# Graph-network kernel, edge-maximum passes: three TensorE signals a step and nine one-hot buffers

## The reference, cut to what matters

```
x = x + attention(relu(layernorm(x)), src, dst)      # stage 1
x = x + pooled_sage(relu(layernorm(x)), src, dst)    # stage 2: two layers
x = x + weighted_sum(relu(layernorm(x)), src, dst)   # stage 3
x = x + propagate(relu(layernorm(x)), src, dst)      # stage 4: 16 steps

# one layer of stage 2 (3125 nodes, 50000 edges sorted by dst, 96 features)
m = relu(x @ Wp + bp)
agg = segment_max(m[src], dst)                       # the edge maximum
return x @ Ws + agg @ Wn + b
```

## Time and profile before

| what | value |
|---|---|
| median of 3 timed runs | 2830.38 us (2829.44 to 2841.82) |
| the profiled execution, its own time | 2817.04 us |
| its span, first to last instruction | 2815.3 us |
| TensorE busy, share of the span | 2462.9 us, 87% |
| VectorE busy | 1766.1 us, 63% |
| ScalarE busy | 1151.0 us, 41% |
| GpSimd busy | 1130.3 us, 40% |
| granted TensorE clock, mean | 0.903 of 2.4 GHz |

### The profile page before, as it was taken

The page is one execution under the profiler, slowest core; times in us unless marked ns, Lnnn a source line. Parts: engine busy times, 40 slices in busy tenths (PEclk is TensorE's granted clock), DMA queues, the critical chain, the costliest instruction groups (busy, mean ns, idle before and its releaser), DMA issues. The chain is left out here.

```text
span 2815.3 us, 72099 instructions
## 1 busy us (share of the span) xinstructions
PE 2462.9 (87%) x29232; PEld 1986.4 (71%) x29232; DVE 1766.1 (63%) x5033; ACT 1151.0 (41%) x2585; POOL 1130.3 (40%) x1407
## 2 busy tenths in 40 slices
PE   6998999986888888677887888469899999999999
PEld 4666777754555555445555565359899999999999
DVE  6997999986777777545776777320444444444444
ACT  5997888864444444423444444310311111111110
POOL 4007999974666666446666666320000000000000
PEclk7558999997999999888998999569999999999999
DMA  5103000013545555533554555549200000000000
GB/s 164 41 2 102 13 12 12 13 61 86 140 127 132 132 131 139 132 96 97 138 133 121 128 140 138 173 146 346 101 2 2 2 2 2 2 2 2 2 2 19
DMA packets 147170, 227.40 MB, mean 81 GB/s; under 512 B 55568, under 2 KB 112619, under 8 KB 146162
## 3 DMA queue, kind: packets, MB, share of 16 engines
q1 hardware_dynamic: 120350, 184.69, 21.8%
q0 software_dynamic: 22944, 36.72, 6.8%
q10 hardware_dynamic: 3540, 1.30, 0.2%
HBM read 122.26 MB, written 100.35 MB: 79 GB/s over the span
## 5 line engine op out<-in xcount | busy, mean ns | idle before, releaser
L1886 POOL DMA_INDIRECT max_row<-table,max_src_rows x640 | 666.5, 1041 | 418.4 <-issue 167.2
L1913 PE MATMUL max_far<-adj 128*96 128x512 f16 x1800 | 546.3, 406 | 8.5 <-issue 7.1
L2035 DVE TENSOR_SCALAR adj<-adj,node_numbers 128x512 f16<-128x512 f16 x900 | 306.0, 352 | 220.4 <-PE max_far L1913 126.2
L1758 POOL TENSOR_SCALAR e<-e 128x512 f32<-128x512 f32 (+1 forms) x625 | 365.8, 604 | 178.5 <-ACT e L1746 160.8
L2380 PE MATMUL prop<-g,adj 128*128 128x192 f16 x4608 | 386.5, 247 | 9.3 <-DVE g L2454 9.3
L1772 DVE TENSOR_TENSOR e<-e,a_ps 128x1024 f32<-128x1024 f32 (+1 forms) x313 | 372.3, 1195 | 32.6 <-PE a_ps L1684 12.7
L2380 PEld LDWEIGHTS prop<-g,adj 128*128 128x128 f16 x4608 | 380.1, 98 | 13.9 <-issue 9.2
L2380 PE MATMUL prop<-weights_then_states,adj 128*128 128x192 f16 x4608 | 384.3, 246 | 0.0
L2380 PEld LDWEIGHTS prop<-weights_then_states,adj 128*128 128x128 f16 x4608 | 378.9, 98 | 3.7 <-issue 2.5
L1746 ACT ACTIVATE e<-s_ps 128x512 f32<-128x512 f32 (+1 forms) x625 | 335.5, 585 | 60.2 <-PE o_ps L1696 38.0
L2488 DVE SCALAR_TENSOR_TENSOR support_parts<-prop,coef,weights_then_states 128x96 f32<-128x96 f32 x384 | 120.5, 314 | 303.9 <-PE prop L2380 226.0
(11 more groups left out here) (287 smaller groups left out, 3514.4 us busy)
## 6 DMA issues: line engine op xcount, KB each, us to landing
weights_then_states<-weights SPq DMA_DIRECT2D x100, 400.0 KB, 5.0
weights<-max_rows_w SPq DMA_DIRECT2D x52, 400.0 KB
rows_dram<-max_out SPq DMA_DIRECT2D x100, 192.0 KB
weights<-adj SPq DMA_DIRECT2D x48, 400.0 KB
max_same<-same_dram SPq DMA_DIRECT2D x196, 96.0 KB
rows_dram<-adj SPq DMA_DIRECT2D x96, 192.0 KB
max_row<-table,max_src_rows POOLq DMA_INDIRECT x640
adj<-ids_dram SPq DMA_DIRECT2D x36, 128.0 KB
```

The source lines that it names most:

```text
L1758: nc.gpsimd.tensor_scalar(e_tile(u), e_tile(u), math.exp(10.0), math.exp(-10.0), ALU.min, ALU.max).then_inc(clipped, 1)
L1886: nc.gpsimd.indirect_dma_start(row[i % RING][:, j, :], None, table_dram, bass.IndirectOffsetOnAxis(ap=src_rows[:, 4 * n + j:4 * n + j + 1] ...
L1913: mm = nc.tensor.matmul(far_ps[j % 2][0:D, :], parts[:, k, a, :], hot[(T * j + k) % HOTS], start=k == a == 0, stop=k == T - 1 and a == 1)
L2035: nc.vector.tensor_scalar(hot[i % HOTS], ids[j % 2], numbers[:, k:k + 1], None, ALU.is_equal).then_inc(hot_made, 1)
```

## The change

TensorE now raises three semaphores and no others. `rows_turned` goes up when the far tile and the turned rows at the head of a step are done, `sums_made` when `lay_out` is done, `step_done` at the end of the step, each only in steps that hold such work. Every wait of another engine goes to the first of the three that comes at or behind the old point, by a count that a table gives (`turned_by`, `back_by`, `laid_by`, `taken_by`, `piece_by`, `wait_far`). So the wait for `back` becomes one for `rows_turned`, those for `hots_used` and `hi_taken` both become `sums_made`, that for `piece_turned` becomes `step_done`, and a one-hot buffer is free at `rows_turned` (a step's first tile), `sums_made` (second and third) or `step_done` (the others).

The one-hot buffers become nine: seven in the old place and two (`hot7`, `hot8`) in memory of their own. And the last strip's four pieces are turned one in each of the last four steps, not two in each of two.

```
-    SAME, LEAD, HOTS, OUTS = 4, 4, 6, 4
+    SAME, LEAD, HOTS, OUTS = 4, 4, 9, 4
+    HOTS_BEHIND = 7
...
-            return [(T - 1, 2 * (m - PARTS) + q) for q in range(2)] if m < PARTS + 2 else []
+            return [(T - 1, m - PARTS)] if m < PARTS + QUARTER else []
...
+        def wait_far(engine, i):
+            m, k = far_at[i]
+            if k < 1:
+                engine.wait_ge(rows_turned, rows_by(m))
+            elif k < 3:
+                engine.wait_ge(sums_made, sums_by(m))
+            else:
+                engine.wait_ge(step_done, ends_by(m))
...
             for m in range(STEPS):
                 tiles = far_tiles(m)
                 if m >= BACK:
-                    turn_back(m - BACK)
-                far(0, 1)
+                    last = turn_back(m - BACK)
+                for j, k in tiles[0:1]:
+                    last = add_far(j, k)
                 if m - LEAD in nth:
-                    turn_rows(m - LEAD)
-                far(1, 2)
+                    last = turn_rows(m - LEAD)
+                if has_rows[m]:
+                    last.then_inc(rows_turned, 1)
+                for j, k in tiles[1:2]:
+                    last = add_far(j, k)
                 if 1 <= m <= PARTS:
-                    take_high(m - 1)
-                far(2, 3)
+                    last = take_high(m - 1)
+                for j, k in tiles[2:3]:
+                    last = add_far(j, k)
                 if m < PARTS:
-                    lay_out(m)
-                far(3, T)
+                    last = lay_out(m)
+                if has_sums[m]:
+                    last.then_inc(sums_made, 1)
+                for j, k in tiles[3:T]:
+                    last = add_far(j, k)
                 for i, q in pieces_of(m):
-                    turn_piece(i, q)
+                    last = turn_piece(i, q)
+                if has_end[m]:
+                    last.then_inc(step_done, 1)
...
             def low_part(n):
-                act.wait_ge(hi_taken, n + 1)
+                act.wait_ge(sums_made, taken_by(n))
...
             def keep_rows(n):
-                act.wait_ge(back, n + 1)
+                act.wait_ge(rows_turned, back_by(n))
```

More of the change, by code:

```diff
@@ L1821, in max_pass @@
         same_loaded = [sem(f"same_loaded{i}") for i in range(SAME)]
-        turned, cleared, scanned, back, kept, zero_out = (
-            sem("turned"), sem("cleared"), sem("scanned"), sem("back"), sem("kept"), sem("zero_out"))
+        rows_turned, cleared, scanned, kept, zero_out = (
+            sem("rows_turned"), sem("cleared"), sem("scanned"), sem("kept"), sem("zero_out"))
         key_hot = [sb(f"key_hot{i}", [P, WIDEST, FEW_KEYS + 3], F16) for i in range(2)]
@@ L1844, in max_pass @@
         behind_parts = pooled_place(adj)[:, T * 2 * D:]
-        hot = [behind_parts[:, BLK * i:BLK * (i + 1)] for i in range(HOTS)]
-        ids = [behind_parts[:, BLK * (HOTS + i):BLK * (HOTS + i + 1)] for i in range(2)]
+        hot = [behind_parts[:, BLK * i:BLK * (i + 1)] for i in range(HOTS_BEHIND)] + [sb(f"hot{i}", [P, BLK], F16)[:, :] for i in range(HOTS_BEHIND, HOTS)]
+        ids = [behind_parts[:, BLK * (HOTS_BEHIND + i):BLK * (HOTS_BEHIND + i + 1)] for i in range(2)]
         ids_loaded = [sem(f"ids_loaded{i}") for i in range(2)]
-        hot_made, hot_used, far_summed, away_loaded = sem("hot_made"), sem("hot_used"), sem("far_summed"), sem("away_loaded")
+        hot_made, away_loaded = sem("hot_made"), sem("away_loaded")
         near = [n for n in range(NB) if n not in FAR]
@@ L1879, in _ @@
                 if i >= RING:
-                    pool.wait_ge(turned, i - RING + 1)
+                    pool.wait_ge(rows_turned, turned_by(near[i - RING]))
                 for j in range(4):
@@ L1903, in turn_rows, with add_far @@
                                               start=a == 0, stop=a == 1, skip_group_check=True)
-                mm.then_inc(turned, 1)
-            def add_far(j, k, used):
+                return mm
+            def add_far(j, k):
                 if k == 0 and j >= 2:
@@ L1928, in lay_out @@
                                               start=w == 0 and h == 0, stop=h == 1, skip_group_check=True)
[L1929 removed]
+                return mm
             def take_high(n):
                 pe.wait_ge(hi_kept, n + 1)
[L1934 to L1935 removed]
+                return nc.tensor.matmul(step_sums(n), minus[:, :], strip_at(0, n),
+                                        start=False, stop=True, skip_group_check=True)
             def turn_piece(i, q):
@@ L1953, in turn_back @@
                     tr = nc.tensor.transpose(back_ps[:, j * D:(j + 1) * D], run[n % 2][:, j:BLK:4], c.ident[0:D, 0:D])
-                tr.then_inc(back, 1)
-            for m in range(NB + BACK):
+                return tr
+            for m in range(STEPS):
                 tiles = far_tiles(m)
-                def far(first, last):
-                    for j, k in tiles[first:last]:
-                        add_far(j, k, 1)
                 if m >= BACK:
-                    turn_back(m - BACK)
-                far(0, 1)
+                    last = turn_back(m - BACK)
+                for j, k in tiles[0:1]:
+                    last = add_far(j, k)
                 if m - LEAD in nth:
-                    turn_rows(m - LEAD)
-                far(1, 2)
+                    last = turn_rows(m - LEAD)
[3 more added lines that the diff above has]
+                    last = add_far(j, k)
                 if 1 <= m <= PARTS:
-                    take_high(m - 1)
-                far(2, 3)
+                    last = take_high(m - 1)
+                for j, k in tiles[2:3]:
+                    last = add_far(j, k)
                 if m < PARTS:
-                    lay_out(m)
-                far(3, T)
+                    last = lay_out(m)
[3 more added lines that the diff above has]
+                    last = add_far(j, k)
                 for i, q in pieces_of(m):
-                    turn_piece(i, q)
+                    last = turn_piece(i, q)
+                if has_end[m]:
+                    last.then_inc(step_done, 1)
         @block.vector
@@ L2000, in weigh @@
                 if n >= 2:
-                    dve.wait_ge(hots_used, n - 1)
+                    dve.wait_ge(sums_made, laid_by(n - 2))
                 dve.wait_ge(lanes_found, n + 1)
@@ L2011, in scan @@
                 if n in nth:
-                    dve.wait_ge(turned, nth[n] + 1)
+                    dve.wait_ge(rows_turned, turned_by(n))
                     cols = col_ps[nth[n] % 2]
                 else:
-                    dve.wait_ge(hot_used, T * (FAR.index(n) + 1))
+                    wait_far(dve, T * (FAR.index(n) + 1) - 1)
                     cols = far_ps[FAR.index(n) % 2]
                 if n >= 2:
-                    dve.wait_ge(back, n - 1)
+                    dve.wait_ge(rows_turned, back_by(n - 2))
                 if n >= 1:
```

39 lines of the change are left out of this document (24 added, 15 removed).

## The result

The changed kernel took 2844.81 us in the median against 2829.54 us of the kernel before, measured beside it. Over the fast runs alone (each kernel had one slow one) the ratio is 1.0049, 95% interval 1.0033 to 1.0064. So it is about 14 us slower. The forecast was 0.95% faster: wrong in its direction, though the time lies in the range. The profiled execution has a span of 2826.7 us.

The account below looks back on a forecast made before the run. It took late TensorE signals, not a full engine, to cost about 208 us in both passes. Terms -35 + 14 - 4 - 2 = -27 us gave 2790, plus 13 us to the median: 2803 us, range 2712 to 2862.

Parts of the forecast that it names:

- What bounds the passes: Both passes: no engine is full; steps take 5.3 us against 4.07 undisturbed, about 208 us lost in all.
- the disturbed step: Step from about 908 us: TensorE's signals arrive three to six us late, then other engines resume within 0.1 us.
- Fewer signals: TensorE's signals in the passes, 928 to about 305 a pass: held-back signals should clear somewhat sooner, -35 us.
- the upper end: Gain if lateness came only from the number of signals: two thirds of the 208 us lost, 140 us.
- the sign that the prediction had named for this: First term wrong if ScalarE's "remote" waits before pieces and strips stay as long in total.
- The attention stage: Evidence against the high end: 4 signals per us against 1.8 in a pass, no "remote" waits, no indirect DMAs.
- Later signals: ScalarE's low part, released 0.79 us later, delays TensorE at a strip's first piece: +14 us, bounds 0 and +40.
- Nine buffers: VectorE's one-hots: most of its 99 us of buffer waits should go, shortening little: 0 to -8 us, taken -4.
- The last strip: Last strip's pieces turned one a step avoid TensorE's wait for ScalarE: -1 us a pass, -2 us.
- the number of signals as most of the lateness: Rival on TensorE's signals in the passes: at least two thirds of 140 us gained, 2690 to 2736 us; chance 0.19.
- The low part is late and nothing else gains: Rival: ScalarE's later low part holds TensorE's first piece of every strip, slower, 2850 to 2875 us; chance 0.27.
- Nothing measurable: Rival: lateness bound to gathers and matmuls, gains lost at the next signal, 2820 to 2840 us; chance 0.15.

Follow-up runs that it names:

- e5: Kernel before with GpSimd's indirect gathers replaced by one plain transfer a near block on SP's queue, from a fixed place: 2551.22 us, ratio 0.9091.
- e3: Kernel before with some 1,215 more signals a pass (2,143 in place of 928), on semaphores nobody waits for: 2804.83 us, ratio 0.9992.
- e7: Kernel before with GpSimd issuing four plain transfers a near block from a fixed place, in place of four indirect gathers: 2552.12 us, ratio 0.9097.
- e8: Kernel before with two of a near block's four indirect gathers replaced by plain transfers, alternating: 2572.26 us, ratio 0.9169.
- e2: Changed kernel with six one-hot buffers kept, so the three signals and the last strip's new order: 2814.77 us, ratio 1.0032.
- e4: Changed kernel with `take_high`'s own signal back and the low part waiting for it: 2808.73 us, ratio 1.0013 to the kernel before.
- e1: Kernel before with nine one-hot buffers in place of six, all ten signals of a step kept: 2815.91 us, ratio 1.0032.
- e12: Kernel before with the memory of two more one-hot buffers taken and never used: 2806.65 us, ratio 1.0006.
- e13: Kernel before with every turned piece moved behind the next step's turned rows, giving the low part more time: 2803.8 us, ratio 0.9984.
- e10: Kernel before with the second of each far tile's two matmuls left out, 450 a pass: 2790.58 us, ratio 0.9951.
- e14: Kernel before with half its gathers plain, each block's two indirect ones first and two plain ones behind: 2572.23 us, ratio 0.9612.

## Why the prediction was wrong

*What bounds the passes.* It read the mechanism off the disturbed step: late signals, then everyone resumes together. That holds where signals are late. The size did not. It put the 208 us lost down to late signals. Sessions without them take 2806 - 2678 = 128 us less; the other 127 us down to the 2551 of the kernel without gathers are what the gathers cost otherwise. GpSimd's own pace can be a part of that: 5.2 us a near block are 419 us a pass, and a pass without gathers takes 389 (e5). The rest is not explained.

*Fewer signals, -35 us.* This is the step that failed. It took a quarter of the upper end on the ground that "given that something holds signals back, a queue with a third of them should clear somewhat sooner". Signals don't hold one another back: more than twice as many change neither time nor lateness (e3), and a third of them were as late (171 against 157 us of ScalarE's waits), the sign that the prediction had named for this. They are late only beside the full stream of indirect gathers (e5, e7, e8), and only in some sessions. The attention stage had spoken for just this, and the prediction overruled it with an argument and no row. The right value was 0, as far as e3 can tell.

*Later signals, +14 us.* About right in size: all coarser signals together cost 9 us (e2, 3 to 15), and e4 gives back 10 us (0 to 22). The place is argued. The waits for the low part went from 7 to 11 in the first body, but all waits at the pieces fell from 46 to 37 us, and in the timeline the rows' late signal holds ScalarE. That signal the prediction put at nothing, since ScalarE is idle before it in an undisturbed step. ScalarE's late waits there grew from 11 to 64 us and TensorE's at `turn_back` from 2.3 to 8.3; no run gave `turn_back` its own signal back, so what this costs is open.

*Nine buffers, -4 us.* Wrong in sign: +0.3%, 9 us (e1, 3 to 14). The prediction saw that "it shortens nothing by itself", and took the freed waits of VectorE to be harmless. Most of them turned up at the scan. Why that costs time rather than none is not shown; memory placement is unlikely (e12) but not excluded.

*The last strip, -2 us,* was not tried alone.

The two halves measured alone, +9 (e1) and +9 (e2), make 18 us against 14 measured. Of the rivals, the number of signals as most of the lateness fell with e3. "The low part is late and nothing else gains" came nearest in direction, but it gave 20 to 45 us, with a margin lost at `take_high` and longer slow stretches on top, and it did not have the loss by the nine buffers. "Nothing measurable" had the cause nearly right (bound to the gathers, and who gains at one wait stands at the next, e13), though not the matmuls: half of the far ones gone leave the lateness as it was (e10).

Three things stay open. One is whether the gathers' number or their standing back to back holds signals up: e8, without lateness beside 2806 us, has both fewer and broken up. Another is what makes one session's signals late and not another's: the kernel is the same, the chip's number 10 stands on both sides, and all sessions with late signals came first. Whether the taking of the trace has a part in it, no run tells; its own events go missing in just those sessions wherever there are gathers (in e8 too). The third is what gains 0.3% without late signals; the change's parts were not run there. No version that does the same work beat the kernel before beside late signals by more than the 0.2% of e13, which its interval doesn't tell from nothing.

## What to carry to other kernels

Where waits are put down to something remote and several engines resume together, ask first what else runs just then, and look for a stage with as many signals and without that neighbour; thinning signals out gained nothing here, and each signal made coarser is a wait made later. Waits on an engine that nobody waits for are no reserve: most of those removed here came back at the scan. And a change of half a per cent had either sign in two sessions, so its verdict holds for the session that it was measured in.

## What the runs showed of the hardware that was not expected

- The same kernel took 2806 us in three sessions (2806.96, 2805.42 and 2805.97, on chips numbered 12, 14 and 10) and 2676 us in three later ones (2677.88, 2675.5 and 2676.36, on chips numbered 0, 10 and 15), 4.6% apart, and 2829.54 us where the change was first measured. In every trace of the later three the signals of TensorE in the passes are on time. With half of the gathers the kernel takes 2572 us in a session of either kind (e8, e14), and without gathers 2551 us in one of the former.
- Where they are late, TensorE's signals come 1.6 to 2.3 us late in the mean (the traces of before and after, e1 to e4 and e10 to e13) and some 5 us in one of ten, while GpSimd issues an indirect gather each 1.3 us. They come at 14 ns beside plain transfers from GpSimd (e7), and on time with every second gather plain (e8).
- An extra semaphore raise on a matmul costs nothing that can be measured: 2,430 of them in both passes, at most 3 us together by e3's interval.
- A GpSimd memset of 128 x 64 between gathers takes 0.20 us, a plain transfer of 128 x 8 there 0.61 us, and an indirect gather 1.04 us plus 0.30 before it.
